# Idle products in TensorE's waits, and a first output projection that waits head by head

## The chip, the cores and the metric

The kernel runs on one core of one Trainium2 chip. The core has five engines, each with a queue of its own: TensorE (PE) multiplies, VectorE (DVE) and ScalarE (ACT) work elementwise, GpSimd (POOL) does the same at a lower pace, SyncE (SP) issues the transfers here. They meet only through semaphores: an instruction adds to one when it is done, another engine waits until it has reached a value. The metric is device time in microseconds (us). The median of three runs before the change is 696.8 us (695.75 to 697.35).

## The reference

A Perceiver layer on 256 tokens of width 512, in three parts, each added to x:

```
x = x + cross_attention(layernorm(x), ctx)   # 16 heads, ctx has 4096 rows of 128
x = x + self_attention(layernorm(x))         # 16 heads, causal, rotary, width 32 + 64
x = x + experts(layernorm(x))                # 32 experts, 4 per token, capacity 10, and a shared one
```

In the cross attention each head's context (256 x 128) is multiplied by w_kc_kv (latent) and the heads' results by Wo, summed over the 16 heads; that sum is the first output projection. The second is that of the self attention. The router takes a sigmoid of the logits, the best three of eight groups, and the best four experts in them.

## The kernel before

All is written by hand: one block of code per engine, in the order in which the engine runs it. Tokens lie in two halves of 128 (TT = 2, index s or st), width 512 in four blocks of 128 (DC = 4).

**Start, to 70 us.** TensorE follows the list PE_BEFORE: for each of eight pairs of heads three products "b" (L941), "a" (L949), "q" (L957), mixed with the transposes of x ("x", L914) and of the context ("rope", L927), the keys ("k", L978 to L980) and products for the maxima ("m", L994). "b0" waits for the first pair of weights; "x" waits for the layer norm, which VectorE (moments, normalised) and ScalarE (root) compute from the loaded x; "q" needs the transposed x, which ScalarE copies (turned_x, L487). VectorE builds the rotated context (rope_rows, L684 to L689) as the pieces of ctx and rope land.

**Cross attention, to 467 us.** Eight times body(): scores, exponentials on ScalarE, context products (L1035, L1036, L1044) into psC, which lies in psO[0]. Per head VectorE copies psC out (head_out, L725, s_out) and GpSimd divides it by the row sum (normalise, L443, ctx_done).

**First output projection (L1095 to L1116).** A loop of H + 2 = 18 steps, staggered: step h transposes head h (L1103), multiplies head h - 1 by wkv (L1109) and head h - 2 by wo1 into psO[0] and psO[1] (L1114), one per token half. ScalarE copies the transposed context (L559), VectorE the latent (L770). The loop starts when all 16 heads are normalised and copied out of psC (the waits at L1095 and L1096).

**Second norm and self attention.** VectorE adds each half to x (residual), takes its moments and normalises (L668, L656 to L664); TensorE transposes (L914) and multiplies (L1124, L1128). Then 21 steps over the 16 heads: queries (L1144 to L1147), scores2 (L1157, L1158), transposes2 (L1164), values2 (L1170 to L1172); VectorE rotates (L783, L784) and takes maxima (L803 to L805), GpSimd adds (L467). At the turn to the second output projection VectorE scales the result (L810), TensorE transposes it (L1187), ScalarE copies it (L599) and TensorE multiplies by wo2 (L1193).

**Third norm, router, experts.** The transposes at L914 again, the logits (L1201), a first piece of the shared expert (L1209), small products for the slots (L1223 to L1225) that wait for the router on VectorE, the gather of tokens (L1231), and eight groups of four experts (gate_up L1255, hidden_back L1265, down L1279, combine L1286).

**Loads.** The expert weights are 1.5 MB each and go through a ring of 13 buffers. Eight experts are loaded from the end of the cross attention on, three more once the first output projection is done (SyncE waits for o1_mm >= H + 1 at L374), two later; each further load waits for a buffer that gate_up or down has freed (L385, L388). The first of these is freed by gate_up(0).

psF[1] is the second half of psS[1], psA[0] the first half of psM.

Of the kernel before, what the change touches and what calls it, by code (L numbers as in the profile page):

```python
# [10 lines left out]
BF16 = mybir.dt.bfloat16  # L11
# [4 lines left out]
P = 128  # L16
T = 256
TT = T // P
# [4 lines left out]
H = 16  # L23
# [34 lines left out]
C_ID, C_MASK, C_EARLY, C_ONES, C_IOTA, C_COS, C_SIN = 0, 128, 512, 640, 768, 784, 1040  # L58
# [22 lines left out]
def order(text):  # L81

    steps = []
    for step in text.split():
# [9 lines left out]
DVE_BEFORE = order("rows0 q0 rows1 rope0 rows2 q1 k0 rows3 q2 rope1 m0 k1 rope2 rope3 k2 m1 m2 q3 k3 m3 m4 m5 q4 k4 m6 m7 m8 q5 "  # L94
                   "k5 m9 m10 k6 m11 m12 q6 m13 k7 m14 m15 q7")
PAIR_BUFS = 6

def expert(k):
# [6 lines left out]
def wait(eng, sem, value):  # L106

    if isinstance(value, int) and value <= 0:
        return
    eng.wait_ge(sem, value)  # L110
# [12 lines left out]
def layer(nc, a, out):  # L123
    with ExitStack() as ctx:
# [6 lines left out]
        def sem(name):  # L131
            return ctx.enter_context(nc.semaphore(name))
# [13 lines left out]
        kt_hi = cut(L // 2).bitcast(BF16)  # L146
# [18 lines left out]
        wo1 = cut(H * D).rearrange("p (h n) -> p h n", h=H)  # L165
# [4 lines left out]
        const = cut(C_END)  # L170
# [22 lines left out]
        latT = arena[:, w_at + 512:w_at + 1024].rearrange("p (b n) -> p b n", b=2)  # L193
# [47 lines left out]
        psO = [ps(f"psO{i}", 512) for i in range(2)]  # L241
        psM = ps("psM", 1024)
        psA = [psM[:, 0:512], psM[:, 512:1024]]
        psE = [psS[0][:, 0:512], psS[0][:, 512:1024]]
        psF = [psS[1][:, 0:512], psS[1][:, 512:1024]]
# [4 lines left out]
        def maxima_bank(q, m):  # L250
# [15 lines left out]
        s_scores, s_phi, s_pf, s_hi, s_pv, s_out = (  # L266
            sem(n) for n in ("s_scores", "s_phi", "s_pf", "s_hi", "s_pv", "s_out"))
# [6 lines left out]
        ctx_done = sem("ctx_done")  # L274
        ct_mm, ct_copied, lat_mm, lat_copied, o1_mm, x1_done = (
            sem(n) for n in ("ct_mm", "ct_copied", "lat_mm", "lat_copied", "o1_mm", "x1_done"))
# [16 lines left out]
            sem(n) for n in ("sh_mm", "sh_silu", "sh_done", "gu_mm", "gu_silu", "hid_done", "hT_mm", "hT_copied",  # L293
                             "y_mm", "y_copied", "comb_mm", "x3_done"))
        sp_passed, pool_passed = sem("sp_passed"), sem("pool_passed")

        block = ctx.enter_context(nc.Block())

# [2 lines left out]
        def _(sp):  # L301
# [69 lines left out]
                load_expert(k, down, ld_down)  # L371
            for k in range(RING_LOW):
                load_whole(k)
            sp.wait_ge(o1_mm, H + 1)  # L374
            for k in range(RING_LOW, RING_MID):
                load_whole(k)
            sp.wait_ge(q2_mm, NH2)
# [261 lines left out]
        def _(dve):  # L639
# [27 lines left out]
            def residual(s, bank, done):  # L667
                nc.vector.tensor_tensor(x[:, s, :], bank[:, :], x[:, s, :], ALU.add).then_inc(done, 1)  # L668
                dve.wait_ge(done, s + 1)
            dve.wait_ge(ld_x, 16)  # L670
            for s in range(TT):
                moments(1, s)
# [97 lines left out]
                nc.vector.tensor_copy(latT[:, h % 2, :], psA[h % 2][:, 0:T]).then_inc(lat_copied, 1)  # L770

            for s in range(TT):
                dve.wait_ge(o1_mm, H + s)
                residual(s, psO[s], x1_done)
                moments(2, s)
            for s in range(TT):
# [15 lines left out]
            for h in range(NH2 + 1):  # L792
# [5 lines left out]
                if h:  # L798
                    g = h - 1
# [76 lines left out]
            for t in range(TT):  # L876
                dve.wait_ge(oh_done, t + 1)
                for rows, width, e0 in ((2 * GE, 3 * CAP, 0), (GE, 2 * CAP, 24)):
                    n = rows * width // CAP
# [28 lines left out]
        def _(pe):  # L908
            mm = nc.tensor.matmul

            def xn_transposed(n, s):
                pe.wait_ge(ln_xn, TT * (n - 1) + s + 1)
                for c in range(DC):
                    last = nc.tensor.transpose(psE[s][:, P * c:P * c + P], xn[:, s, P * c:P * c + P], ident)  # L914
                last.then_inc(ln_tr, 1)

            def xn_transposes(n):
                for s in range(TT):
                    xn_transposed(n, s)

            def rope_transposes(n):
                pe.wait_ge(kr_done, n + 1)
# [169 lines left out]
            body(NPAIR - 1, LAST)  # L1092
            context_lo(NPAIR - 1, SLOTS - 1)

            pe.wait_ge(ctx_done, H)  # L1095
            pe.wait_ge(s_out, H)  # L1096
            pe.wait_ge(ld_wkv, 16)
            pe.wait_ge(ld_wo1, 16)
            for h in range(H + 2):
                if h < H:  # L1100
                    wait(pe, ct_copied, h - 1)
                    for st in range(TT):
                        last = nc.tensor.transpose(psS[0][:, 512 * (h % 2) + P * st:512 * (h % 2) + P * st + P], ctx_all[:, st, h, :], ident)  # L1103
                    last.then_inc(ct_mm, 1)
                if 1 <= h <= H:
                    g = h - 1
                    pe.wait_ge(ct_copied, g + 1)
                    wait(pe, lat_copied, g - 1)
                    mm(psA[g % 2][:, 0:T], wkv[:, g, :], ctxT[:, g % 2, :], start=True, stop=True).then_inc(lat_mm, 1)  # L1109
                if h >= 2:  # L1110
                    g = h - 2
                    pe.wait_ge(lat_copied, g + 1)
                    for st in range(TT):
                        last = mm(psO[st][:, :], latT[:, g % 2, P * st:P * st + P], wo1[:, g, :], start=g == 0, stop=g == H - 1)  # L1114
                        if st == TT - 1 or g == H - 1:
                            last.then_inc(o1_mm, 1)  # L1116

            xn_transposes(2)
            pe.wait_ge(ln_T, 2 * TT)
            pe.wait_ge(ld_wa, 16)  # L1120
            pe.wait_ge(lat_copied, H)
            for n, w in enumerate((w_qa, w_kva)):
                for c in range(DC):
                    last = mm(psA[n][:, 0:T], w[:, c, :], xnT[:, c, :], start=c == 0, stop=c == DC - 1)  # L1124
                last.then_inc(qa_mm, 1)
            pe.wait_ge(x1_done, TT)
            for c in range(DC):
                last = mm(psO[0][:, 0:T], w_kpe[:, c, :], xnT[:, c, :], start=c == 0, stop=c == DC - 1)  # L1128
# [4 lines left out]
            def values():  # L1133
                for st in range(TT):
                    mm(psF[st][:, :], ckv[:, P * st:P * st + P], w_vb, start=True, stop=True).then_inc(v_mm, 1)
# [31 lines left out]
            def values2(h):  # L1167
                pe.wait_ge(pT_copied, h + 1)
                w = slice(V2 * h, V2 * h + V2)
                mm(psO[0][:, w], pT[:, h % 2, 0:P], v2[:, 0, w], start=True, stop=True)  # L1170
                mm(psO[1][:, w], pT[:, h % 2, P:2 * P], v2[:, 0, w], start=True, stop=False)
                mm(psO[1][:, w], pT[:, h % 2, 2 * P:3 * P], v2[:, 1, w], start=False, stop=True).then_inc(o2_mm, 1)  # L1172
            for h in range(NH2 + 5):
                if h < NH2:
                    queries(h)
                if h == 0:
                    values()
                if 0 <= h - 1 < NH2:
                    scores2(h - 1)
                if 0 <= h - 3 < NH2:  # L1180
                    transposes2(h - 3)
                if 0 <= h - 4 < NH2:
                    values2(h - 4)
            for st in range(TT):
                pe.wait_ge(o2_done, st + 1)
                for c in range(DC):
                    last = nc.tensor.transpose(psS[0][:, T * c + P * st:T * c + P * st + P], xn[:, st, P * c:P * c + P], ident)  # L1187
            last.then_inc(o2T_mm, 1)
            pe.wait_ge(o2T_copied, 1)
            pe.wait_ge(ld_wo2, 16)  # L1190
            for st in range(TT):
                for c in range(DC):
                    last = mm(psA[st][:, :], xnT[:, c, P * st:P * st + P], wo2[:, c, :], start=c == 0, stop=c == DC - 1)  # L1193
# [4 lines left out]
            for st in range(TT):  # L1198
                pe.wait_ge(ln_T, 2 * TT + st + 1)
                for c in range(DC):  # L1200
                    last = mm(psA[0][:, E * st:E * st + E], xnT[:, c, P * st:P * st + P], w_router[:, c, :], start=c == 0, stop=c == DC - 1)  # L1201
# [26 lines left out]
            for c in range(DC):  # L1228
                wait(pe, xp_copied, c - 1)
                for st in range(TT):  # L1230
                    last = mm(psE[c % 2][:, 0:E * CAP], xn[:, st, P * c:P * c + P], oh[:, st, :], start=st == 0, stop=st == TT - 1)  # L1231
# [156 lines left out]
```

## Time and profile before

| | |
|---|---|
| median of three runs | 696.8 us (695.75 to 697.35) |
| the profiled execution | 695.87 us |
| its span | 694.0 us |
| mean granted clock of TensorE | 0.975 |
| TensorE busy | 631.8 us (91%) |
| VectorE busy | 386.7 us (56%) |
| ScalarE busy | 360.5 us (52%) |
| GpSimd busy | 187.5 us (27%) |
| chain that ended last | PE 63%, DVE 14%, issue 10%, DMA 4%, SP's queue 4%, ACT 4% |

### The profile page before, as it was taken

Reading aid. Unit: us, or ns where it says so; the run is one execution under the profiler, and the core shown is the slowest. Engines: PE = TensorE matmul, PEld = TensorE weight load, DVE = VectorE, ACT = ScalarE, POOL = GpSimd, SP = SyncE. Lnnn points to the kernel's source line nnn. Section 1 sums busy time; section 2 is a strip of 40 time slices with the busy share of each in tenths; the row PEclk is TensorE's granted clock in tenths of the full one; section 3 lists DMA queues with packets and bytes.
Section 4 is the critical chain, followed back from the end, with each engine's and each line's share of the span. In section 5 each row is a group of like instructions: output and inputs, shape, how many; then the busy total and the mean of one; then the engine's idle time right before and its main releaser. Section 6 shows DMA issues by size and latency. Waiting matters only on the chain.

```text
span 694.0 us, 14831 instructions
## 1 busy us (share of the span) xinstructions
PE 631.8 (91%) x5841; PEld 457.0 (66%) x5892; DVE 386.7 (56%) x536; ACT 360.5 (52%) x517; POOL 187.5 (27%) x151
## 2 busy tenths in 40 slices
PE   6999899999999999999999999999978988899855
PEld 5977666777777777777777777985546875553211
DVE  4869587767767677767677766341136854300001
ACT  3532766667666676667666766861126862110000
POOL 0250333443344334433442444440002220000000
PEclk9999999999999999999999999999989997999989
DMA  9934964324315305206215224009970051199993
GB/s 353 418 112 86 282 206 92 64 42 98 73 25 112 72 9 128 59 12 133 47 28 120 46 45 105 2 8 405 418 302 35 0 211 64 44 418 418 418 417 132
DMA packets 25511, 105.13 MB, mean 151 GB/s; under 512 B 3968, under 2 KB 7296, under 8 KB 19584
## 3 DMA queue, kind: packets, MB, share of 16 engines
q1 hardware_dynamic: 25472, 104.57, 46.1%
q8 instruction: 29, 0.48, 0.3%
q14 instruction: 10, 0.08, 0.0%
HBM read 77.29 MB, written 0.52 MB: 112 GB/s over the span
## 4 chain that ended last, share of the span: by engine, by line
PE 63%; DVE 14%; issue 10%; DMA 4%; SPq 4%; ACT 4%; POOL 1%; DVEq 0%; ACTq 0%
DVE arena L744 8%; PE psO L1044 6%; PE psM L994 6%; PE psO L1035 5%; PE psO L1036 5%; PE psS L1022 5%; PE psS L1023 5%; PE psO L1114 4%; SPq L366 4%; PE psO L979 3%; DMA arena<-w_exp 3%; PE psO L949 2%; PE psS L1255 2%; PE psS L957 2%; PE psO L980 2%
## 5 line engine op out<-in xcount | busy, mean ns | idle before, releaser
L707 DVE TENSOR_REDUCE arena<-psM 128x2 f32<-128x1024 f32 x121 | 148.3, 1225 | 80.9 <-PE psM L994 80.6
L425 POOL TENSOR_TENSOR arena<-arena 128x1024 bf16<-128x1024 f32 x64 | 138.4, 2163 | 147.5 <-ACT arena L531 143.5
L530 ACT ACTIVATE arena<-psS 128x1024 bf16<-128x1024 f32 x128 | 132.3, 1033 | 26.0 <-PE psS L1023 13.7
L1035 PE MATMUL psO<-arena 128*128 128x129 bf16 x1024 | 132.8, 220 | 1.5 <-ACT arena L530 1.2
L531 ACT ACTIVATE arena<-psS 128x1024 f32<-128x1024 f32 x128 | 132.6, 1036 | 0.0
L1036 PE MATMUL psO<-arena 128*128 128x128 bf16 x1024 | 132.3, 220 | 0.0
L1022 PE MATMUL psS<-arena 128*128 128x256 bf16 x512 | 120.5, 273 | 0.9 <-DVE arena L718 0.9
L1023 PE MATMUL psS<-arena 65*128 65x256 bf16 x512 | 120.8, 273 | 0.0
L1035 PEld LDWEIGHTS psO<-arena 128*128 128x128 bf16 x1024 | 99.1, 98 | 20.9 <-issue 12.7
L1036 PEld LDWEIGHTS psO<-arena 128*128 128x128 bf16 x1024 | 99.4, 97 | 6.7
L744 DVE TENSOR_TENSOR arena<-arena 128x1024 bf16<-128x1024 f32 x64 | 82.2, 1285 | 20.8 <-ACT arena L531 20.8
L522 ACT CAST arena<-psO 128x512 bf16<-128x512 f32 x64 | 37.6, 588 | 101.2 <-PE psO L980 101.2
L1044 PE MATMUL psO<-arena 128*128 128x129 bf16 x1024 | 79.9, 221 | 4.4 <-DVE arena L744 1.0
L1044 PEld LDWEIGHTS psO<-arena 128*128 128x128 bf16 x1024 | 61.8, 97 | 19.1 <-DVE arena L744 18.4
L1022 PEld LDWEIGHTS psS<-arena 128*128 128x128 bf16 x512 | 50.2, 98 | 7.0 <-DVE arena L642 1.0
L1023 PEld LDWEIGHTS psS<-arena 65*128 65x128 bf16 x512 | 50.0, 98 | 5.4
L994 PE MATMUL psM<-arena 64*128 64x512 bf16 x242 | 47.2, 386 | 3.0 <-DVE arena L707 2.8
L701 DVE TENSOR_TENSOR arena<-psO,arena 128x512 bf16<-128x512 f32 x64 | 44.0, 688 | 9.9 <-ACT arena L522 6.4
L1255 PE MATMUL psS<-arena 128*32 128x512 f32 x256 | 32.4, 652 | 12.5 <-DMA arena<-w_exp 12.0
L894 DVE TENSOR_TENSOR arena<-psS,arena 128x256 f32<-128x256 f32 x8 | 3.4, 425 | 69.6 <-ACT arena L606 69.6
L606 ACT ACTIVATE arena<-psS 128x256 f32<-128x256 f32 x8 | 3.1, 385 | 60.7 <-PE psS L1255 60.7
L467 POOL TENSOR_TENSOR arena<-arena 64x256 f32<-64x256 f32 x16 | 11.5, 720 | 82.2 <-DVE arena L784 82.2
(188 smaller groups left out, 743.5 us busy)
## 6 DMA issues: line engine op xcount, KB each, us to landing
arena<-w_exp SPq DMA_DIRECT2D x32, 1024.0 KB, 17.1
arena<-arena SPq DMA_DIRECT2D x96, 256.0 KB, 3.8
arena<-w_exp SPq DMA_DIRECT2D x32, 512.0 KB, 17.9
arena<-w_pair SPq DMA_DIRECT2D x8, 1088.0 KB, 16.4
arena<-w_o SPq DMA_DIRECT2D x1, 4096.0 KB, 18.4
arena<-ctx SPq DMA_DIRECT2D x4, 512.0 KB, 12.9
arena<-rope SPq DMA_DIRECT2D x4, 512.0 KB, 13.6
arena<-w_shared_in SPq DMA_DIRECT2D x1, 2048.0 KB, 8.4
```

What stands on the lines that cost most here:

```text
L425: nc.gpsimd.tensor_tensor(p_lo[:, s % 2, :], p_f[:, s % 2, :], p_hi[:, s % 2, :], ALU.subtract).then_inc(s_plo[0], 1)
L530: nc.scalar.activation(p_hi[:, s % 2, :], psS[s % 2][:, :], ACT.Exp).then_inc(s_phi, 1)
L531: nc.scalar.activation(p_f[:, s % 2, :], psS[s % 2][:, :], ACT.Exp).then_inc(s_pf, 1)
L707: nc.vector.reduce_max(maxes[:, :, st, c], maxima_bank(q, m)[:, :].rearrange("p (j n) -> p j n", j=2), AX.X).then_inc(s_mfree, 1)
L744: nc.vector.tensor_tensor(p_lo[:, s % 2, :], p_f[:, s % 2, :], p_hi[:, s % 2, :], ALU.subtract).then_inc(s_plo[1], 1)
L994: last = mm(bank[:, 512 * j:512 * j + 512], queries_of[r, P * st:P * st + P], k_hi[r, 512 * c:512 * c + 512], start=True, stop=True)
L1022: mm(o, k1[:, j, l], q1[:, j, :], start=True, stop=False)
L1023: last = mm(o, k2[0:R + 1, j, l], q2[0:R + 1, j, :], start=False, stop=True)
L1035: mm(psC[:, st, :], ph, vx[:, GROUP * g + i, 0:CW], start=g == 0 and i == 0 and st == 0, stop=False, skip_group_check=True)
L1036: last = mm(psC[:, st, 0:K], ph, vx[:, GROUP * g + i, CW:VW], start=False, stop=False, skip_group_check=True)
L1044: last = mm(psC[:, st, :], p_lo[:, s % 2, T * i + P * st:T * i + P * st + P], vx[:, GROUP * g + i, 0:CW], start=False, stop=g == HALF - 1 ...
L1255: last = mm(psF[g % 2][SLOT * j:SLOT * j + SLOT, :], xpT[:, c, CAP * e:CAP * e + SLOT], ring[k % RING][:, 2 * FI * c:2 * FI * (c + 1)], st ...
```

## The change

Three things are done.

- **Idle products.** A function warm(n, bank, of) issues n bf16 products of 128 weights by 512 columns, into a PSUM bank that nobody reads then. Operands are two constants: kt_hi[:, 0:512], filled with ones by VectorE at the start, later 512 bf16 columns' worth of the constants table. There are 14 at the very start, 13 before the second norm's transposes, 3 each at steps 2 and 3 of the self-attention loop (before scores2), 4 before and 4 behind the transposes at L1187, and 9 between the transposes of the two token halves for the third norm.
- **Waits of the first output projection.** Step h waits for head h alone (ctx_done >= h + 1); the wait for VectorE's copy of the last psC (s_out) stands before the first product into psO.
- **The last two heads.** The products of heads 14 and 15 by wo1 are taken after the last latent copy, first both heads for token half 0, then both for half 1. o1_mm ends at H = 16, not H + 1, and the two waits on it (SyncE, VectorE) are lowered by one.

```diff
+WARM_START, WARM_NORM, WARM_HEADS, WARM_TURN, WARM_LAST = 14, 13, 3, 4, 9
...
-            sp.wait_ge(o1_mm, H + 1)
+            sp.wait_ge(o1_mm, H)
...
+            nc.vector.memset(kt_hi[:, 0:512], 1.0).then_inc(warm_ready, 1)
             dve.wait_ge(ld_x, 16)
...
-                dve.wait_ge(o1_mm, H + s)
+                dve.wait_ge(o1_mm, H - 1 + s)
...
+            def warm(n, bank, of=const[:, C_EARLY:C_EARLY + 256].bitcast(BF16)):
+
+                for _ in range(n):
+                    mm(bank[:, 0:512], of[:, 0:P], of[:, 0:512], start=True, stop=True)
+            pe.wait_ge(warm_ready, 1)
+            warm(WARM_START, psF[1], kt_hi)
+
...
                 for s in range(TT):
                     xn_transposed(n, s)
+                    if n == 3 and s == 0:
+                        warm(WARM_LAST, psF[1])
...
-            pe.wait_ge(ctx_done, H)
-            pe.wait_ge(s_out, H)
             pe.wait_ge(ld_wkv, 16)
             pe.wait_ge(ld_wo1, 16)
+            def projected(g, st):
+                return mm(psO[st][:, :], latT[:, g % 2, P * st:P * st + P], wo1[:, g, :], start=g == 0, stop=g == H - 1)
             for h in range(H + 2):
                 if h < H:
                     wait(pe, ct_copied, h - 1)
+                    pe.wait_ge(ctx_done, h + 1)
...
-                if h >= 2:
+                if 2 <= h < H:
                     g = h - 2
                     pe.wait_ge(lat_copied, g + 1)
+                    if g == 0:
+                        pe.wait_ge(s_out, H)
                     for st in range(TT):
-                        last = mm(psO[st][:, :], latT[:, g % 2, P * st:P * st + P], wo1[:, g, :], start=g == 0, stop=g == H - 1)
-                        if st == TT - 1 or g == H - 1:
-                            last.then_inc(o1_mm, 1)
-
+                        last = projected(g, st)
+                    last.then_inc(o1_mm, 1)
+            pe.wait_ge(lat_copied, H)
+            for st in range(TT):
+                for g in (H - 2, H - 1):
+                    last = projected(g, st)
+                last.then_inc(o1_mm, 1)
+
+            warm(WARM_NORM, psF[1])
             xn_transposes(2)
...
+                if h in (2, 3):
+                    warm(WARM_HEADS, psM[:, 0:512])
                 if 0 <= h - 1 < NH2:
                     scores2(h - 1)
...
+            warm(WARM_TURN, psF[1])
             for st in range(TT):
                 pe.wait_ge(o2_done, st + 1)
...
             last.then_inc(o2T_mm, 1)
+            warm(WARM_TURN, psF[1])
             pe.wait_ge(o2T_copied, 1)
```

## Rows read from the trace of the kernel before

**Rows 1.** The page, granted TensorE clock in 40 slices, tenths of full speed.
```profile
PEclk9999999999999999999999999999989997999989
```

**Rows 2.** Windows of 1 us: busy per engine, clock, DMA; first and last low.
```profile
471.00:472.00 1.00, 1.00 (x3) 0.48 (x3) 0.42 (x1) 0.00 (x0) 0.00 (x0) 0.50 0.91 375
...
587.00:588.00 1.00, 1.00 (x4) 0.81 (x3) 0.91 (x3) 1.00 (x1) 0.00 (x0) 0.50 0.00 0
```

**Rows 3.** Chain of waits in time order: start us, duration us, what.
```profile
26.89 0.22 PE psO L980
...
471.14 3.16 PE psO L1114 x4
...
474.95 1.72 PE psO L1114 x4
...
658.01 21.25 DMA arena<-w_exp
```

**Rows 4.** Timeline of SyncE's queue at the end: start, duration, line.
```profile
603.95 61.16 SPq L366 DMA_DIRECT2D arena<-w_exp  x40
```

**Rows 5.** Timeline of TensorE, first 40 us: start, duration, line, [idle before].
```profile
5.79 2.82 PE L941 MATMUL psS<-arena 128*128 128x64 f32 x12 [5.79 <-DMA arena<-w_pair]
...
15.11 3.75 PE L957 MATMUL psS<-arena 128*128 128x256 f32 x8 [0.77 <-ACT arena L487]
...
18.66 2.07 PE L941 MATMUL psS<-arena 128*128 128x64 f32 x12
...
24.52 1.95 PE L957 MATMUL psS<-arena 128*128 128x256 f32 x8
...
34.36 1.50 PE L941 MATMUL psS<-arena 128*128 128x64 f32 x12
```

**Rows 6.** Timeline of VectorE, first 35 us.
```profile
11.31 0.55 DVE L664 TENSOR_SCALAR arena<-arena 128x512 f32<-128x512 f32 x1
...
29.57 1.28 DVE L684 TENSOR_TENSOR arena<-arena 128x512 f32<-128x512 f32 x2
```

**Rows 7.** Timeline of SyncE's queue at the start.
```profile
8.05 1.90 SPq L310 DMA_DIRECT2D arena<-rope  x1
```

**Rows 8.** Line 310, its four transfers: issue to landing.
```profile
DMA to landing us min/median/max: 7.3/13.6/19.1
```

**Rows 9.** Timeline of TensorE, 466 to 600 us.
```profile
468.64 0.66 PE L1103 MATMUL psS<-arena 128*128 128x128 f32 x4 [1.41 <-POOL arena L443]
...
505.37 3.60 PE L1114 MATMUL psO<-arena 128*128 128x512 f32 x8
...
512.41 1.97 PE L914 MATMUL psS<-arena 128*128 128x128 f32 x8 [3.44 <-DVE arena L664]
...
515.05 5.30 PE L1124 MATMUL psM<-arena 128*128 128x256 f32 x16 [0.68 <-ACT arena L487]
...
532.01 1.22 PE L1144 MATMUL psM<-arena 128*128 128x256 f32 x2 [0.75 <-ACT arena L571]
...
568.86 1.72 PE L1187 MATMUL psS<-arena 128*128 128x128 f32 x8 [0.85 <-DVE arena L810]
...
571.68 9.42 PE L1193 MATMUL psM<-arena 128*128 128x512 f32 x16 [1.10 <-ACT arena L599]
...
584.03 0.66 PE L914 MATMUL psS<-arena 128*128 128x128 f32 x4 [2.49 <-DVE arena L664]
...
586.27 5.39 PE L1209 MATMUL psS<-arena 128*128 128x256 f32 x16
...
592.26 0.41 PE L1223 MATMUL psM<-arena 128*128 128x32 f32 x2 [0.60 <-DVE arena L830]
...
595.15 4.57 PE L1231 MATMUL psS<-arena 128*128 128x320 f32 x16 [2.03 <-DVE arena L874]
```

**Rows 10.** Timeline of VectorE, 500 to 540 us.
```profile
505.57 0.42 DVE L770 COPY arena<-psM 128x256 f32<-128x256 f32 x1 [1.72 <-PE psM L1109]
...
534.98 0.42 DVE L783 TENSOR_TENSOR arena<-psS,arena 64x256 f32<-64x256 f32 x1 [2.63 <-PE psS L1147]
```

More of the change, by code:

```diff
@@ L295, in layer @@
         sp_passed, pool_passed = sem("sp_passed"), sem("pool_passed")
+        warm_ready = sem("warm_ready")
         block = ctx.enter_context(nc.Block())
```

## The prediction

> **What bounds the kernel now.** I read the page's clock row first [rows 1]: TensorE's granted clock is full in nearly every slice, so the low stretches are short and have to be looked for one microsecond at a time. Windows of 1 us show five of them between 470 us and 590 us, at the lower of the two levels (0.50, that is 1.2 GHz); the first and the last stand in [rows 2]. The others begin near 511.5, 531.9 and 569.5 us. Every one begins just after a stretch in which TensorE waited for another engine. Then I read the chain of waits, in order of time [rows 3], for whether such a stretch lies on the path: four output products on the same tile take 3.16 us in the low stretch and 1.72 us right after it, and both stand in the chain. Last, the chain ends in a wait for expert weights: these loads are issued one behind the other from the first that gate_up(0) frees [rows 4], and the chain's last DMA piece, 21.25 us long, ends at 679.3 [rows 3], so the last 80 us are set by when they start, 603.95 us. Whatever makes 603.95 earlier makes the end earlier; what happens on TensorE behind it is hidden.
>
> The start is low too, and there the clock row doesn't show it (its first slice reads 9 [rows 1]). The durations do [rows 5]: the twelve passes of the first b product take 2.82 us, the same twelve later 1.50; the eight of the q product 3.75 and later 1.95.
>
> The Trainium skill, "TensorE: Matmul & The Clock Gate", section "Part 1: The HAM clock gate (the "warmup" mystery)", says that the throttle events in a profile can't be fully trusted and are to be held against durations. This trace agrees, 2.82 us under a clock row of 9. By the clock row alone the start would bring nothing and the sum would be 2.5 us smaller.
>
> **Prices.** At the higher level one pass of 512 columns takes 0.43 us in f32 (1.72 us for 4) and 0.22 us in bf16 (L980) [rows 3]; one of 256 f32 columns is then 0.22 us (the eight of the q product take 1.95 with the end of the last [rows 5]) and one of 128 0.11 us. At the lower level each doubles. An idle product is one bf16 pass of 512 columns: 0.22 us, or 0.43 us at the lower level. No row shows these in place, so both are kept as its bounds.
>
> **Part 1, 14 idle products at the start.** TensorE waits until 5.79 us for the first pair of weights [rows 5]. The products wait only for a fill of 512 columns on VectorE and can begin near 0.9 us (the first load is issued at 0.73). At the lower level they take 6.0 us, to 6.9, so b0 starts up to 1.1 us late. It then takes 1.5 in place of 2.82 and ends near 8.4, not 8.6; the a product behind it (sixteen such passes, 2.0 us) ends by 10.7. The transposes of x then wait for VectorE (11.31 + 0.55 = 11.9 us [rows 6]) and not for TensorE: the last ends at 12.3, ScalarE's copy keeps TensorE for 0.77 as before [rows 5], and the q product starts near 13.1 in place of 15.11. That is 2.0 us, and 0.5 more as the b product behind it was partly low (2.07 for 1.50). TensorE and VectorE then run tightly to 70 us, so 2.5 us stay, if data are there. The last quarter of the rotation table is issued at 8.05 [rows 7] and lands at most 19.1 us later [rows 8], at 27.2; VectorE takes it at 29.57 [rows 6]: 2.4 us of slack. Bounds: 1.1 us lost (the clock doesn't rise) and 4.3 us won (the q product at full clock too, 1.8 more). I take **-2.5**, with the q product still low: what runs before it is short. The fill on VectorE is done before x lands.
>
> **Part 2, the wait head by head.** Before the output projection TensorE waits 1.41 us for GpSimd's last normalise, at 468.64 us [rows 9], though heads 0 to 14 are ready. Now the transposes start right away; the wait for head 15 comes fifteen heads later, over 30 us after its work is done. The wait for VectorE's copy of psC moves in front of the first product into psO. That copy starts with the end of the last context product and would be done while the first two heads are transposed and multiplied. **-1.4**. What is queued behind both waits is the same work as before.
>
> The low stretch 470.5 to 473.9 follows from that wait [rows 2]. It costs 3.16 - 1.72 = 1.44 us on four products and 0.3 on a smaller one between. With 1.4 us less idle time I take it as gone: **-1.7** (bounds 0 and -1.7). Four transposes stand at its beginning, 0.66 us [rows 9]; at 512.41 eight ran low, after a wait of 3.44 us. The Trainium skill, "TensorE: Matmul & The Clock Gate", section "Part 4: PE-mode transpose", says that transposes don't count as activity in the way of other products. By that rule the stretch might stay low and the sum would be 1.7 us smaller; this trace can't decide it, since the wait alone could have caused what it shows.
>
> **Part 3, the last two heads by halves.** Before, head 14's products covered VectorE's copy for head 15 (505.57 + 0.42 [rows 10]). Now TensorE waits for it until about 506.1, then does half 0 of both heads (1.7 us, to 507.8) and half 1 (to 509.5). Before, the first half was done at 505.37 + 2.6 = 507.9, the second at 508.97 [rows 9]. VectorE takes the second half only after about 1.8 us of work on the first, 509.7. **-0.1**. SyncE's wait (H, no longer H + 1) falls on the same last product, 0.5 us later, with expert loads behind it that are not used before 600 us.
>
> **Part 4, 13 products before the second norm.** TensorE sits 3.44 us before 512.41 [rows 9]. The products fill 13 x 0.22 = 2.8 us, from 509.5 to 512.3: just hidden. What follows was low: eight transposes 1.97 us for about 1.0, and sixteen passes in 5.30 us [rows 9] for 16 x 0.22 = 3.5. **-2.8** (bounds: +2.7 if they run at the lower level, from 509.5 to 515.1; -2.8).
>
> **Part 5, 3 products at heads 2 and 3.** They are hidden: 0.65 us each, before scores that wait for VectorE and GpSimd or end with slack to VectorE. The low stretch at 531.9 made the three products from 532.01 [rows 9] to VectorE's 534.98 [rows 10] take 2.97 us; at full clock they take 3 x 0.43 + 0.1 = 1.4. **-1.5** (bounds +0.3, -1.5). After that VectorE is the bound at every head.
>
> **Part 6, 4 and 4 products at the turn.** The first four, 0.9 us, fill the 0.85 us gap before 568.86, the second four the 1.10 us gap before the second output projection [rows 9]. The eight transposes go from 1.72 to about 1.0 us, the sixteen passes from 9.42 to 16 x 0.43 = 6.9. **-3.2** (bounds +1.4, -3.2).
>
> **Part 7, 9 products between the last transposes.** 2.0 us in a gap of 2.49 us before 584.03 [rows 9]: hidden. Behind them, the shared product at 586.27 took 5.39 us at mostly low clock [rows 9], 3.5 at full, but it isn't what the router waits for. VectorE's router steps are. So **0**, and here something is given back. TensorE now ends it 1.9 us sooner, near 589.8 by the old times, and has then only six short passes from 592.26 on until 595.15 [rows 9]: some 4.5 us of waiting in 5.4, more than preceded any stretch above. The clock falls, and the 16 gather passes at 595.15 (4.57 us, on the path before gate_up(0)) start low. If they run low for 3.4 us, as the short stretch from 470.5 to 473.9 did, half of that is lost: **+1.7** (bounds 0 and +4.3, all sixteen at half clock).
>
> **Sum:** -2.5 - 1.4 - 1.7 - 0.1 - 2.8 - 1.5 - 3.2 + 1.7 = -11.5. The profiled execution took 695.87 us (694.0 span, 1.9 around it), so 684.4. The median of the three runs, 696.8, lies 0.9 above that execution. I put some half of that, 0.4, on top: **684.8 us**. The rivals' times start from there.
>
> **Rivals.**
> - Only some stretches stay high (chance 0.22). Places of low stretches may shift in an earlier program. If the hand-over stays low (1.7), half of the turn's gain goes (1.6) and 1.0 at the start, the time is 689.1. For it: the gaps at the turn carry only short products. Against: each gap is nearly filled.
> - The start is swallowed (0.1): if the loads decide and not the q product, 2.5 less: 687.3. For it, the 2.4 us of slack [rows 6 to 8] are all there is; against it, nothing at the start waits for a load after 5.79 us.
> - More given back at the router (0.1): all sixteen gather passes low, 2.6 more: 687.4. For it, nothing heavy precedes them; against it, a short stretch ends after 3.4 us of work.
> - Slower (0.04): the idle products don't raise the clock and stand, at 0.43 us each, before real work. +1.1 at the start, +2.7 before the norm, +0.3 at the heads, +0.85 and +0.6 at the turn, +1.4 at the last transposes, -1.5 for the hand-over: +5.4 on 695.9 and the 0.4, 701.7. It decides as soon as the norm's thirteen run low. Against it: plain products alone bring the clock back at 474 us.
> - No effect (0.02), 696.3: the loads at the end start by something other than gate_up(0). Against it, [rows 4].
>
> **How the numbers follow.** The forecast has 0.52. Its own bounds are 681.3 (start 4.3, nothing given back) and 687. With the two rivals near 687 and most of the first, 680.5 to 690.5 holds about 0.85. A measurement here tells about 0.2% (1.4 us) from no change. Every case but the last two is faster: 0.94, same 0.02, slower 0.04.
>
> **What would show it.** The first q product near 13 us; the first transpose of the projection right behind the last context product; no low clock from 464 to 582 us; the 16 passes of L1124's products in about 3.5 us and those of L1193's in 6.9; a low stretch between 589 and 599 us that wasn't there; the first w_exp load behind gate_up(0) near 592 us; an unchanged length from there to the end, about 90 us. I am wrong if low stretches remain in those places, if the q product starts after 15, or if that last part gets longer.

## The result, and the profile after

The changed kernel takes 686.64 us (685.26 to 687.77) against 696.98 before: a ratio of 0.9855, 95% interval 0.9836 to 0.9874, 10.3 us in the medians. In a second set of runs it took 685.46 against 695.93, 0.9852 (0.9828 to 0.9876). The forecast was 684.8 us, range 680.5 to 690.5. The profiled execution took 686.27 us, span 684.4, 9.6 less than the span before; stage by stage below, the forecast's sum of -11.5 is set against that. Two single executions, one of the kernel before (1,236.6 us) and one of e11 (1,251.0 us), are left out of the ratios; they move no median given here by more than 0.1 us, and their cause is open.

First the page's row of the granted clock, 40 slices of 17 us, against [rows 1].

```profile
PEclk9999999999999999999999999999999999899989
```

Then TensorE's timeline of the changed kernel (start, duration, line, passes, idle time before them). L917 is the idle product; L969 was L957, L1116 L1103, L1122 L1109, L1110 L1114, L924 L914, L1144 L1124, L1148 L1128, L1164 L1144, L1192 L1172, L1210 L1187, L1217 L1193, L1233 L1209, L1247 L1223, L1255 L1231, L1279 L1255. In what follows the clock is called low where it is 0.50 and full where it is 1.00.

```profile
1.46 5.96 PE L917 MATMUL psS<-arena 128*128 128x512 bf16 x14 [1.46 <-DVE arena L672]
...
13.48 1.97 PE L969 MATMUL psS<-arena 128*128 128x256 f32 x8 [0.77 <-ACT arena L489]
...
464.56 0.61 PE L1116 MATMUL psS<-arena 128*128 128x128 f32 x4
...
466.62 1.98 PE L1110 MATMUL psO<-arena 128*128 128x512 f32 x4
...
499.24 0.59 PE L1122 MATMUL psM<-arena 128*128 128x256 f32 x2
500.35 3.70 PE L1110 MATMUL psO<-arena 128*128 128x512 f32 x8 [0.52 <-DVE arena L773]
503.89 2.97 PE L917 MATMUL psS<-arena 128*128 128x512 bf16 x13
506.70 1.26 PE L924 MATMUL psS<-arena 128*128 128x128 f32 x8
508.63 3.72 PE L1144 MATMUL psM<-arena 128*128 128x256 f32 x16 [0.67 <-ACT arena L489]
...
524.00 0.70 PE L1164 MATMUL psM<-arena 128*128 128x256 f32 x2 [0.75 <-ACT arena L573]
...
558.20 1.03 PE L917 MATMUL psS<-arena 128*128 128x512 bf16 x4
559.22 1.25 PE L1210 MATMUL psS<-arena 128*128 128x128 f32 x8
560.31 1.03 PE L917 MATMUL psS<-arena 128*128 128x512 bf16 x4
561.57 7.13 PE L1217 MATMUL psM<-arena 128*128 128x512 f32 x16 [0.24 <-ACT arena L601]
...
571.64 0.66 PE L924 MATMUL psS<-arena 128*128 128x128 f32 x4 [0.55 <-DVE arena L666]
...
573.88 3.70 PE L1233 MATMUL psS<-arena 128*128 128x256 f32 x16
579.87 0.41 PE L1247 MATMUL psM<-arena 128*128 128x32 f32 x2 [2.28 <-DVE arena L833]
...
582.75 6.83 PE L1255 MATMUL psS<-arena 128*128 128x320 f32 x16 [1.97 <-DVE arena L877]
```

Held against [rows 5] and [rows 9], two kinds of change are to be seen. The passes on the path have become short: the q product 3.75 to 1.97 us, the four first output passes 3.36 (3.16 in the chain, [rows 3]) to 1.98, L1144 5.30 to 3.72, L1217 9.42 to 7.13. And one has become long: the gather L1255, 4.57 to 6.83, behind two waits of 2.28 and 1.97 us. Windows of 1 us of the changed kernel show that this is the clock: where [rows 2] had 0.50 at 471 us there is 1.00, and between 455 and 600 us it is low from 580.5 to 587.3 only.

```profile
471.00:472.00 1.00, 1.00 (x6) 0.71 (x5) 0.34 (x1) 0.37 (x1) 0.00 (x0) 1.00 1.03 434
...
584.00:585.00 1.00, 1.00 (x3) 0.65 (x2) 0.00 (x0) 0.00 (x0) 0.00 (x0) 0.50 0.00 0
```

SyncE's queue of the changed kernel issues the first freed expert load at 593.80 us, before it was 603.95 [rows 4]; the chain's last DMA piece is as long as in [rows 3].

```profile
593.80 46.56 SPq L368 DMA_DIRECT2D arena<-w_exp  x32
```

```profile
648.31 21.31 DMA arena<-w_exp
```

The first place in the table below is VectorE's bias rows, a copy of 512 elements on one partition just before the scores. The line of the kernel before, then that of the changed one:

```profile
70.73 0.69 DVE L718 CAST arena<-psO 1x512 bf16<-1x512 f32 x1
```

```profile
68.25 0.69 DVE L721 CAST arena<-psO 1x512 bf16<-1x512 f32 x1
```

How much earlier than before each place is reached, in the two profiled executions:

| place | before | after | earlier | by this stage | forecast |
|---|---|---|---|---|---|
| VectorE's bias rows, start of the scores | 70.73 | 68.25 | 2.48 | -2.5 | -2.5 |
| last product by wkv | 504.94 | 499.24 | 5.70 | -3.2 | -3.1 |
| first residual on VectorE | 508.14 | 502.38 | 5.76 | -0.1 | -0.1 |
| end of the first products after the norm (L1148 starts) | 520.19 | 512.19 | 8.00 | -2.2 | -2.8 |
| last products of the heads (L1192) | 567.62 | 557.98 | 9.64 | -1.6 | -1.5 |
| first transposes for the third norm | 580.93 | 568.54 | 12.39 | -2.8 | -3.2 |
| gather starts | 595.15 | 582.75 | 12.40 | 0.0 | 0 |
| first freed expert load | 603.95 | 593.80 | 10.15 | +2.3 | +1.7 |
| end of the span | 694.0 | 684.4 | 9.6 | +0.5 | 0 |

### The profile page after: what moved, and what is told of

It reads as the page before. It is cut to its first block, busy times and chain, and to the rows that moved or that the text cites. A ratio compares the mean times of both kernels' runs of the same rounds, so it can differ in the third digit from the quotient of the medians.

```text
span 684.4 us, 14997 instructions
## 1 busy us (share of the span) xinstructions
PE 640.5 (94%) x5942; PEld 452.3 (66%) x5942; DVE 388.1 (57%) x537; ACT 360.0 (53%) x517; POOL 188.8 (28%) x151
## 4 chain that ended last, share of the span: by engine, by line
PE 62%; DVE 15%; issue 9%; DMA 6%; ACT 4%; SPq 2%; POOL 1%; DVEq 0%; ACTq 0%
DVE arena L747 8%; PE psO L1056 7%; PE psM L1006 6%; PE psO L1047 5%; PE psO L1048 5%; PE psS L1034 5%; PE psS L1035 5%; PE psO L1110 4%; PE psS L1279 3%; DMA arena<-w_exp 3%; DMA arena<-rope 3%; PE psO L990 3%; PE psO L992 2%; PE psO L991 2%; DVE arena L710 2%
## 5 line engine op out<-in xcount | busy, mean ns | idle before, releaser
L1056 PEld LDWEIGHTS psO<-arena 128*128 128x128 bf16 x1024 | 61.8, 97 | 19.1 <-DVE arena L747 18.3
L1279 PE MATMUL psS<-arena 128*32 128x512 f32 x256 | 32.6, 655 | 12.9 <-DMA arena<-w_exp 12.3
L469 POOL TENSOR_TENSOR arena<-arena 64x256 f32<-64x256 f32 x16 | 11.5, 719 | 75.1 <-DVE arena L787 75.1
```

The source lines that it names most:

```text
L1056: last = mm(psC[:, st, :], p_lo[:, s % 2, T * i + P * st:T * i + P * st + P], vx[:, GROUP * g + i, 0:CW], start=False, stop=g == HALF - 1 ...
L1279: last = mm(psF[g % 2][SLOT * j:SLOT * j + SLOT, :], xpT[:, c, CAP * e:CAP * e + SLOT], ring[k % RING][:, 2 * FI * c:2 * FI * (c + 1)], st ...
```

## The experiments

All go from the changed kernel; WARM_ counts stand in the order start, norm, heads, turn, last. The position of a stage is read in each one's profile, and "from the bias rows" is a distance from VectorE's bias rows (near 68 us). A and B are theory A and rival B of the expectation above each result. A profile shows one execution, a time is the median of several.

**The waits alone** (e1). All counts 0, so the idle products are left out.

```diff
-WARM_START, WARM_NORM, WARM_HEADS, WARM_TURN, WARM_LAST = 14, 13, 3, 4, 9
+WARM_START, WARM_NORM, WARM_HEADS, WARM_TURN, WARM_LAST = 0, 0, 0, 0, 0
```

> The changed kernel with all idle products left out (counts 0): only the head-by-head waits and the halves stay. Theory A (each group of idle products keeps the clock for the work behind it, the hand-over stays at full clock because its wait is gone): start as before the change (first q product at 15.1 us, low), the four output products behind the hand-over in 1.7 us, low stretches back before L1144, at the heads and at the turn. Worth 3.2 us against the kernel before: 693.8. Rival B (the clock at the hand-over is held by the warm past, not by the shorter wait; with transposes first it falls as before): the low stretch near 470 us stays and the gain is 1.4 us: 695.5.

694.38 us (690.78 to 696.24); ratio 0.9976, interval 0.9948 to 1.0003. In the median it is no clear gain, in the trace (of an execution of 693.29 us) the waits do what was forecast. TensorE's timeline of this kernel:

```profile
466.25 0.63 PE L1056 MATMUL psO<-arena 128*128 128x129 bf16 x8 [0.51 <-DVE arena L747]
466.71 0.61 PE L1116 MATMUL psS<-arena 128*128 128x128 f32 x4
...
502.51 3.70 PE L1110 MATMUL psO<-arena 128*128 128x512 f32 x8 [0.52 <-DVE arena L773]
...
508.80 1.31 PE L924 MATMUL psS<-arena 128*128 128x128 f32 x8 [2.59 <-DVE arena L666]
...
510.78 5.29 PE L1144 MATMUL psM<-arena 128*128 128x256 f32 x16 [0.67 <-ACT arena L489]
...
567.39 9.42 PE L1217 MATMUL psM<-arena 128*128 128x512 f32 x16 [1.10 <-ACT arena L601]
...
675.27 6.58 PE L1279 MATMUL psS<-arena 128*32 128x512 f32 x32 [5.10 <-DMA arena<-w_exp]
```

The transposes stand right behind the last context product, and the clock is full through the hand-over: A, not B, in this execution. The low stretches at the norm, the heads, the turn and in the shared product are back. That at the norm is shorter than before the change: the eight transposes ran nearly full (1.31 us), the sixteen passes of L1144 low (5.29).

Why so little of it is left in the median is shown in part. At the first freed expert load the profiled execution is 4.3 us ahead of the kernel before (599.65 against 603.95), at its end only 2.5, since the last expert group (L1279) took 6.58 us for 4.97. And the ten runs fall in two groups: five took 690.8 to 693.6 us at a mean granted clock of 0.978 to 0.980, five 695.2 to 696.2 us at 0.973 to 0.977. No profile shows where the second group was low, so that the hand-over stayed full there too isn't shown.

**The products alone** (e2). The first projection as in the kernel before.

```diff
+            pe.wait_ge(ctx_done, H)
+            pe.wait_ge(s_out, H)
...
-                    pe.wait_ge(ctx_done, h + 1)
...
-                    if g == 0:
-                        pe.wait_ge(s_out, H)
```

> The idle products alone, with the first output projection, its waits and o1_mm counts as in the kernel before. Theory A: the wait of 1.4 us and a low stretch of 3.4 us behind it are back, everything else as in the changed kernel: 3.2 us slower than it, near 689.9, 7 us faster than before the change. Rival B (the low stretch was a matter of where it fell in time): the four output products take 1.7 us though the wait is there; only 1.4 us slower than the changed kernel.

689.19 us (687.08 to 690.04), ratio 0.9899 (0.9866 to 0.9933). TensorE's timeline again shows the wait and the slow passes:

```profile
465.91 0.66 PE L1115 MATMUL psS<-arena 128*128 128x128 f32 x4 [1.41 <-POOL arena L445]
...
468.37 3.20 PE L1126 MATMUL psO<-arena 128*128 128x512 f32 x4
```

So the low stretch there hangs on the wait of 1.41 us, as theory A has it: it is there in both profiles with the wait (the kernel before, e2) and in none of the eleven without it. The products alone bring 6.5 us in the medians (695.66 to 689.19), the waits on top of them some 3 (689.19 against 686.64 and 685.46).

**No products at the start** (e4): WARM_START = 0, no products before the first load.

> The changed kernel without the 14 products at the start. Theory A: first q product back at 15.1 us and low (3.75 us for 8 passes), scores of the first pair start 2.5 us later (near 71.6 us), 689.1. Rival B (the loads set the pace of the start in any case, and the products only moved waits): less than 1 us slower than the changed kernel, VectorE's first scores operand (L721) before 69.3 us.

687.9 us (687.11 to 688.72), ratio 0.9886 (0.9845 to 0.9927). The q product is back at 15.09 us and 3.75 us long, VectorE's bias rows at 70.59: 2.3 us later than with them, A. In the medians it is 1.3 to 2.4 us slower than the changed kernel's two. What limits these 2.5 us the other executions show by themselves. In one (e5) the q product ran 3.65 us, mostly low, at 13.12; in the nine others with these products it started anywhere from 12.45 to 13.48 and ran 1.97 us. The bias rows were at 67.85 to 68.25 in all ten, and at 68.06 in e5. So the q product no longer sets them. VectorE's timeline of the changed kernel names what does:

```profile
17.06 2.36 DVE L687 TENSOR_TENSOR arena<-arena 128x512 f32<-128x512 f32 x2 [0.53 <-DMA arena<-rope]
...
23.50 1.29 DVE L687 TENSOR_TENSOR arena<-arena 128x512 f32<-128x512 f32 x2 [0.29 <-DMA arena<-rope]
...
28.72 1.29 DVE L687 TENSOR_TENSOR arena<-arena 128x512 f32<-128x512 f32 x2 [0.36 <-DMA arena<-rope]
```

Three of its four context pieces now wait for the rotation table to land; none did before. In the nine profiles that have these products and a full q product the bias rows follow the start of the fourth piece (28.72 here) by 39.53 or 39.54 us, in e5 by 39.89: where the last quarter of the table lands decides the start. But that fourth piece begins only 0.85 us earlier than before (29.57 [rows 6]). The other 1.6 us come behind it, where VectorE had waited for TensorE's products for the maxima. VectorE's line of the kernel before, then that of the changed one, which waits no more:

```profile
36.23 1.23 DVE L707 TENSOR_REDUCE arena<-psM 128x2 f32<-128x1024 f32 x1 [1.27 <-PE psM L994]
```

```profile
34.04 1.22 DVE L710 TENSOR_REDUCE arena<-psM 128x2 f32<-128x1024 f32 x1
```

**No products at the norm** (e5): WARM_NORM = 0.

> The changed kernel without the 13 products before the second norm's transposes. Theory A: TensorE waits 3.0 us again and the sixteen passes of L1144 take 5.3 us in place of 3.72; the eight transposes may run low too. From the residual at L670 to the end of L1144 it takes 1.6 to 2.3 us longer: 688.5 in all. Rival B (what the products give here goes again at the heads, where VectorE sets the pace): under 0.7 us slower.

688.65 us (688.53 to 688.76), ratio 0.989 (0.9858 to 0.9922), 2.0 above the changed kernel. TensorE's timeline of this kernel:

```profile
508.49 5.20 PE L1144 MATMUL psM<-arena 128*128 128x256 f32 x16 [0.68 <-ACT arena L489]
```

From the bias rows to L1148 it is 1.5 us longer than with the products (513.53 - 68.06 against 512.19 - 68.25). A in its kind, just short of its 1.6 to 2.3; the turn was low in this execution too. All 1.5 us lie in L1144. From the first residual to L1144 it is 6.25 us here as with the products (508.49 - 502.24), and in e1 too (510.78 - 504.53), so the 0.7 us that went there don't come from these 13.

**No products at the heads** (e6): WARM_HEADS = 0.

> The changed kernel without the 3 and 3 products at heads 2 and 3. Theory A: a low stretch of 3.4 us is back near 524 us, the three products before VectorE's wait take 3.0 us in place of 1.4, and the loop of heads is 1.5 us longer: 688.1. Rival B (where the low stretch falls at the heads depends on the moment and mostly lies beside VectorE's work): under 0.5 us slower, 686.9.

685.99 us (685.04 to 687.28), ratio 0.9857 (0.9822 to 0.9892): no slower than with them. VectorE's timeline of this kernel, whose first operation after the wait was at 534.98 after 2.63 us before the change [rows 10]:

```profile
525.30 0.42 DVE L786 TENSOR_TENSOR arena<-psS,arena 64x256 f32<-64x256 f32 x1 [1.26 <-PE psS L1167]
```

With the products it is at 525.60, also after 1.26 us. No low stretch came back without them: B in the time. In e5 the norm was low and these products were there, and from L1148 to the last L1192 it took 45.8 us as in the changed kernel. In e1, where the norm was low and they were missing, the stretch is there (L1164 1.22 us at 527.73) and it took 47.4. So either was enough here; each case stands on one profile.

**No products at the turn** (e7): WARM_TURN = 0.

> The changed kernel without the 4 and 4 products at the turn. Theory A: transposes and second output projection low for 6.8 us as before the change, 16 passes of L1217 in 9.4 us in place of 7.13: 2.8 us slower, 689.4. Rival B (one execution of the kernel with these products already had the first four of them low, so they don't hold the clock but only bring its return forward): slower by 1 to 1.6 us, 687.9.

687.75 us (686.58 to 688.3), ratio 0.9874 (0.984 to 0.9908), 1.1 to 2.3 us slower than the changed kernel's two medians: nearer to B. The 16 passes took 8.70 us. Its low stretch lasted 6.8 us (558.3 to 565.1), as A says; in each of the five profiles that have the products and were low at the turn it lasted 3.4. From the last L1192 to the last transposes for the third norm and the router (L1225) it took 16.4 us without the products, 15.4 to 15.5 with them where the turn was low, and 14.2 where it was full. So they bring 1.0 or 2.3 us, by execution.

**No products between the last transposes** (e8): WARM_LAST = 0.

> The changed kernel without the 9 products between the last transposes. My prediction gave them 0. Theory A (a shared product at full clock ends sooner and leaves TensorE waiting, so the gather starts low; these 9 are what keeps it full): without them L1233 runs low for 3.4 us where nobody waits for it, the gather L1255 is back at 4.6 us, and the kernel is 2.2 us FASTER than with them, 684.4. Rival B (the clock falls before the gather in any case): L1255 stays at 6.8 us and the time at 686.6.

686.85 us (686.65 to 689.17), ratio 0.9876 (0.9839 to 0.9912): no faster. TensorE's timeline has the shared product low (5.20 us), as A says, and the gather low again (6.26 us), as B says:

```profile
575.17 5.20 PE L1233 MATMUL psS<-arena 128*128 128x256 f32 x16
...
583.92 6.26 PE L1255 MATMUL psS<-arena 128*128 128x320 f32 x16 [2.03 <-DVE arena L877]
```

A low shared product ahead of the gather doesn't by itself keep the gather full. A's conclusion fell. Over all profiles without products before the gather: where the shared product ran full and TensorE then waited 2.28 to 2.30 us before L1247, the gather was low in seven of seven; where it ran low and the wait was 0.60 to 0.67 us, in one of four (this one; not in the kernel before, e1 and e10).

**Products before the gather** (e3), to test the loss at the router.

```diff
             shared_hidden(0)
+            warm(8, psF[1])
             pe.wait_ge(sel_done, 1)
...
+            warm(7, psF[1])
             pe.wait_ge(oh_done, TT)
```

> The changed kernel with 8 more idle products in front of TensorE's wait for the router (sel_done) and 7 in front of its wait for the one-hot tiles (oh_done). Theory A (the low stretch from 580.8 to 587.8 us comes from TensorE finishing the shared product sooner and then waiting): the gather L1255 takes 4.6 us in place of 6.83, the first freed expert load goes out 2.2 us sooner and the end moves as much: 684.4. Rival B (the sixteen short and transposing passes before it are what drops the clock, or the loads at the end take the gain back): gather still above 6 us, or the stretch from the first freed load to the end grows by 2 us: 686.6.

685.53 us (684.8 to 687.33), ratio 0.9864 (0.9821 to 0.9906). TensorE's timeline:

```profile
557.98 1.76 PE L917 MATMUL psS<-arena 128*128 128x512 bf16 x4
559.53 1.92 PE L1210 MATMUL psS<-arena 128*128 128x128 f32 x8
...
574.86 5.39 PE L1233 MATMUL psS<-arena 128*128 128x256 f32 x16
580.09 1.89 PE L917 MATMUL psS<-arena 128*128 128x512 bf16 x8
...
583.91 4.55 PE L1257 MATMUL psS<-arena 128*128 128x320 f32 x16
```

The gather is at full clock, A. But the turn went low, with its four idle products before the transposes at 0.43 us each, and this ate half of it.

**The changed kernel again** (e10), unaltered, for comparison with the three that follow.

> The changed kernel unaltered, as the measure for the three kernels beside it on the same chip: 686.6.

685.46 us (685.23 to 686.23). Its profile has the same span as the first, 684.4 us, by another way. TensorE's timeline:

```profile
559.52 1.92 PE L1210 MATMUL psS<-arena 128*128 128x128 f32 x8
...
574.85 5.39 PE L1233 MATMUL psS<-arena 128*128 128x256 f32 x16
...
583.73 4.58 PE L1255 MATMUL psS<-arena 128*128 128x320 f32 x16 [2.03 <-DVE arena L877]
...
668.25 6.52 PE L1279 MATMUL psS<-arena 128*32 128x512 f32 x32 [5.17 <-DMA arena<-w_exp]
```

The same code, but low at the turn (from 558.0) and in the shared product, full in the gather, and the last expert group, on the path behind the last load, takes 6.52 us where the first execution had 5.07. So one profile gives the place of a low stretch only for itself. The last group of the first execution:

```profile
669.76 5.07 PE L1279 MATMUL psS<-arena 128*32 128x512 f32 x32 [4.93 <-DMA arena<-w_exp]
```

In the nine profiles whose turn has its four and four products and nothing else new ahead of it, the clock was low there in five (e3, e5, e8, e10, e12). In the nine that have idle products, but none right before the gather, the gather was low in eight (all but e10).

**Six and six before the gather** (e11), as e3 with counts 6 and 6.

> The changed kernel with 6 more idle products before the router's wait and 6 before the wait for the one-hot tiles (8 and 7 were one or two too many: the gather started 0.2 us late). Theory A (the gather's low stretch comes from TensorE's waiting): gather in 4.6 us, 2.2 us faster than the changed kernel, 684.4. Rival B (the clock before the gather depends more on the moment than on these products): gains below 1 us in the median.

684.08 us (682.71 to 685.89), ratio 0.9828 (0.9807 to 0.985): 1.4 us faster than e10, between A's 2.2 and B's less than 1. Its profile is of the execution of 1,251.0 us, so no row is read from it, and that the gather was full isn't shown for these counts alone.

**And three at the last head steps** (e9): the six and six before the gather, twelve at the norm, three at step 18.

```diff
+                if h == 18:
+                    warm(3, psM[:, 512:1024])
                 if h in (2, 3):
```

> The same 6 and 6 before the gather, 12 in place of 13 before the second norm, and 3 new idle products at step 18 of the self-attention loop, before the last transposes2, where TensorE waits 0.67 us for ScalarE. Theory A (the turn was low in three of seven executions because little but short products runs just before it, so more work there holds the clock): no low stretch at the turn, 1 us faster than the changed kernel with 6 and 6 alone in the median, 683.6. Rival B (it falls there by the moment anyway): the same time as with 6 and 6 alone, 684.4.

683.56 us (683.48 to 684.49), ratio 0.9832 (0.9811 to 0.9853). It is the fastest version; all its runs lie below all of e10's. The clock is full in every window from 455 to 600 us. TensorE's timeline:

```profile
558.83 1.25 PE L1212 MATMUL psS<-arena 128*128 128x128 f32 x8
...
561.18 7.13 PE L1219 MATMUL psM<-arena 128*128 128x512 f32 x16 [0.24 <-ACT arena L601]
...
582.37 4.57 PE L1259 MATMUL psS<-arena 128*128 128x320 f32 x16 [0.74 <-DVE arena L877]
```

Against e11 it is 0.5 us, within the spread of the runs, so what step 18 adds isn't shown, only that this execution had neither stretch.

**The old order of the last two heads** (e12).

```diff
-                if 2 <= h < H:
+                if h >= 2:
...
+                        if st == TT - 1 or g == H - 1:
+                            last.then_inc(o1_mm, 1)
```

> The changed kernel with the last two heads in the old order (head 14 both halves, then head 15 both halves; o1_mm ends at H + 1 again). Theory A (the halves trade 0.5 us of waiting for one product less before VectorE's first half): within 0.2 us of the changed kernel, the first residual 3.2 us after the last L1122 in place of 3.14. Rival B (TensorE, which is the bound from there through the idle products, loses 0.5 us by the halves): 0.5 us faster than the changed kernel.

687.04 us (685.4 to 687.47), ratio 0.9866 (0.9844 to 0.9889), whose interval holds e10's ratio of 0.9852. The first residual starts 3.21 us after the last L1122 (502.35 - 499.14) in place of 3.14, and the transposes 7.48 in place of 7.46: A by place, the halves are worth 0.1 us at the most there. By time the expectation missed: the median is 1.6 us above e10's, not within 0.2. The profiled execution was low at turn and gather both; whether the order has to do with that isn't shown.

## Why the prediction was right, step by step

- **Start, -2.5: the size was right, half of its reason was not.** I had the q product still low at 13.1 us, and a gain of 4.3 if it ran full. It started at 13.48 and ran full, and still 2.5 us came out. The idle products began at 1.46, not 0.9: I had left out the fill itself, which takes 0.48 us from 0.92. The rival "the loads decide" had the mechanism, and its price (nothing left) was wrong. My 2.4 us of slack were wrong too: the table's last quarter landed 20.6 us after its issue, not 19.1, and the piece that waits for it gained 0.85 us; 1.6 us more came from VectorE's wait for TensorE behind it. That 2.4 and the measured 2.5 lie so near is chance.
- **Hand-over, -1.4 and -1.7: right**, 3.2 measured. e1 and e2 show both halves. By the rule of the Trainium skill ("TensorE: Matmul & The Clock Gate", section "Part 4: PE-mode transpose") the stretch might have stayed low. With the same four transposes first and the wait gone, none of eleven profiles has it.
- **Halves, -0.1: right** by place (0.06, and e12's profile).
- **Norm, -2.8: mis-sized, 2.2 measured.** The term that failed is the 1.0 us for the eight transposes. The path goes by the second four, which wait for VectorE's second tile (506.70 + 0.55, so 507.3), and the copies behind them. From the first residual to L1144 only 0.7 us went (6.91 to 6.25). The other 1.6, in L1144, came nearly as forecast (1.8). And the 0.7 came without the thirteen products too (e1, e5), so it isn't theirs. Two of the low stretches that I said begin just after a wait, near 511.5 and 531.9, begin in it.
- **Heads, -1.5: the size was right (1.6), the cause not as I put it.** The three and three products weren't needed where the norm before had a full clock (e6); where it hadn't, the stretch was full with them (e5) and low without (e1). Which of the earlier products, or the mere shift in time, keeps it full there is open.
- **Turn, -3.2: 2.8 in that execution, less on the mean.** The step up to the passes of L1217 gave 0.5, not 0.7 (the transposes took 1.25, not 1.0), the passes 2.3, not 2.5 (7.13, not 6.9). What I counted into a rival of chance 0.22 (half of the turn's gain goes) happens in five of nine profiles. By my own sign of being wrong, a low stretch left in such a place, this step failed in e10, which is the same code.
- **Router, +1.7: right, 2.3 measured.** It is low for 6.8 us, not 3.4, so the forecast was 0.6 short; in e3 and e9, with products in the waits, the loss is gone.
- **After the first freed load, 0: 0.5 lost.** Between it and the end lie 90.0 to 91.9 us in the profiles here; most of that spread is the last L1279 (4.97 us before, 5.07 after, 6.52 in e10, 6.58 in e1), which starts after 5 us of waiting for a load and which I left out though it is on the path. The 0.5 here is another thing: from the first freed load to the start of the last L1279 it took 75.96 us (669.76 - 593.80), before 75.45. Why is open.

The sum, -11.5, was 1.9 us too large for the profiled span (norm 0.6, turn 0.4, router 0.6, end 0.5, less 0.2). The 0.4 us from the profiled execution to the median came out as assumed (686.64 against 686.27).

## What to carry to other kernels

A low clock stretch costs half of what lies on the path (at the hand-over 1.7 us of 3.4), and the wait before it can be taken away or filled; taking away a wait (here one condition asked fifteen heads too early) gives twice, its own length and the slow passes behind it. Before filling, look for the next wait: work that ends sooner makes a longer one further down, and the clock can fall there instead (before the gather, 0.60 us became 2.28, and the gather took 6.83 us in place of 4.57). Read where low stretches lie from several profiles, not from one, and price an idle product from both levels: at the lower one it takes double and stands before real work.

## What the runs showed of the hardware

- Before the change, the profile of the start says full clock (1.00) while the passes take nearly twice their later time (3.75 against 1.95 us for eight); only durations tell there. After 14 idle products (5.96 us, 0.43 each) the b product ran at its full-clock time, 1.45 us.
- Idle bf16 products of 512 columns take 0.22 us each at 2.4 GHz (2.97 us for 13 with the last one's end) and 0.43 at 1.2 GHz.
- Two executions of one program, both of 684.4 us span, had their low stretches between 455 and 600 us in different places: 580.5 to 587.3 in one, 558.0 to 561.5 and 575.1 to 578.5 in the other. So the code alone doesn't decide it.
- Over nine profiles with the same products at the turn, of kernels that differ elsewhere, the turn was low in five. What decides it is open.
